# A query bias copied into three of four PSUM banks by ScalarE, with TensorE's bias product kept for the fourth

## What is computed

```
q = softmax(x @ Wq.T + bq, over the 16 channels of a head)
k = softmax(x @ Wk.T + bk, over the 1024 tokens)
v = x @ Wv.T + bv
state = einsum('bhnd,bhne->bhde', k, v);  out = einsum('bhnd,bhde->bhne', q, state)
out = layernorm(out) @ Wo.T + bo
x1 = layernorm(x + out)
```

## Time and profile before

| what | value |
|---|---|
| median of 3 executions | 569.5 us (569.3 to 569.98) |
| the profiled execution's own time | 569.85 us |
| its span | 568.0 us, 10876 instructions |
| DVE, ACT, POOL busy | 502.9, 483.1, 402.7 us |
| PE's granted clock, mean | 0.991 |
| DMA | 46.52 MB, mean 82 GB/s |

### The profile page before, as it was taken

One profiled execution on the slowest core, in us unless ns is written; L12 is line 12 of the kernel. 1 busy time (PEld: TensorE's weight loads), 2 busy tenths in 40 slices (PEclk: granted clock), 3 DMA queues, 4 the chain that ended last, 5 costly groups with the idle time before them and its releaser, 6 DMA issues.

```text
span 568.0 us, 10876 instructions
## 1 busy us (share of the span) xinstructions
PE 541.4 (95%) x3542; PEld 494.0 (87%) x3542; DVE 502.9 (89%) x1276; ACT 483.1 (85%) x951; POOL 402.7 (71%) x390
## 2 busy tenths in 40 slices
PE   6999999999999999988899999999999999999990
PEld 6899999898999989878788998888899888899890
DVE  5888898988899898857587999999999999999986
ACT  4655689799989878877989999999999999999983
POOL 4782979877797987575458776876676776675672
PEclk9999999999999999999999999999999999999996
DMA  8540040230705020250111012222112222100102
GB/s 294 198 149 2 1 186 39 82 141 9 289 1 224 1 113 38 76 200 24 75 38 39 38 37 76 75 74 76 44 33 75 76 74 76 59 18 37 39 38 111
DMA packets 11399, 46.52 MB, mean 82 GB/s; under 512 B 1360, under 2 KB 1744, under 8 KB 9168
## 3 DMA queue, kind: packets, MB, share of 16 engines
q1 hardware_dynamic: 10912, 45.29, 21.9%
q10 hardware_dynamic: 432, 0.54, 0.3%
HBM read 29.02 MB, written 16.81 MB: 81 GB/s over the span
## 4 chain that ended last, share of the span: by engine, by line
PE 74%; DVE 11%; ACT 8%; DMA 2%; issue 2%; POOL 1%; ACTq 0%; DVEq 0%; POOLq 0%
PE ring L1874 20%; PE qps_sps_aps_then_y L1898 20%; PE qps_sps_aps_then_y L1745 7%; PE qps_sps_aps_then_y L1659 7%; PE ring L1687 5%; PE qps_sps_aps_then_y L1764 5%; PE ring L1816 2%; DVE z L1177 2%; PE ring L1791 2%; DVE qsum L1071 1%; PE ring L1779 1%; PE ring L1829 1%; PE qps_sps_aps_then_y L1720 1%; ACT z L746 1%; DMA w_raw<-in_wq_dram 1%
## 5 line engine op out<-in xcount | busy, mean ns | idle before, releaser
L1898 PE MATMUL qps_sps_aps_then_y<-ff_w_over_xc_lo,ff_a_lo_over_qw 128*128 128x258 f32 x512 | 126.5, 283 | 0.0
L1898 PE MATMUL qps_sps_aps_then_y<-ff_w_over_xc_lo,ff_a_hi_over_xc_lo 128*128 128x258 f32 x512 | 126.4, 283 | 0.0
L1874 PE MATMUL ring<-ff_ht_hi_over_qw,t 128*128 128x512 f32 x256 | 105.6, 412 | 0.9 <-DVE ff_ht_lo_over_xc_hi L1249 0.5
L1874 PE MATMUL ring<-ff_ht_lo_over_xc_hi,t 128*128 128x512 f32 x256 | 100.8, 394 | 0.0
L1898 PEld LDWEIGHTS qps_sps_aps_then_y<-ff_w_over_xc_lo,ff_a_hi_over_xc_lo 128*128 128x128 f32 x512 | 96.9, 189 | 3.5
L1898 PEld LDWEIGHTS qps_sps_aps_then_y<-ff_w_over_xc_lo,ff_a_lo_over_qw 128*128 128x128 f32 x512 | 96.7, 189 | 3.4
L1257 DVE SCALAR_TENSOR_TENSOR ff_a_lo_over_qw<-ring,ff_rho,ff_a_hi_over_xc_lo 128x512 fp32r<-128x512 f32 x128 | 91.5, 742 | 5.7 <-ACT ff_a_hi_over_xc_lo L807 4.5
L789 ACT ACTIVATE ring<-ring,bias 128x512 f32<-128x512 f32 x128 | 84.1, 677 | 11.2 <-PE ring L1874 10.2
L522 POOL TENSOR_TENSOR ff_accp_over_xt_lo<-ff_accp_over_xt_lo,ff_sq_over_ek_et_hi 128x512 f32<-128x512 f32 x64 | 84.3, 1317 | 4.7
L805 ACT ACTIVATE ff_sq_over_ek_et_hi<-ring 128x512 f32<-128x512 f32 x128 | 79.1, 618 | 0.5
L807 ACT CAST ff_a_hi_over_xc_lo<-ring 128x512 fp32r<-128x512 f32 x128 | 78.0, 609 | 0.0
(11 more groups left out here) (179 smaller groups left out, 1631.1 us busy)
## 6 DMA issues: line engine op xcount, KB each, us to landing
x_scratch<-z SPq DMA_DIRECT2D x16, 514.0 KB, 2.9
ff_x_over_w_raw_xc<-x_scratch SPq DMA_DIRECT2D x16, 514.0 KB, 4.8
xt<-in_x_tok_dram SPq DMA_DIRECT2D x8, 1024.0 KB, 4.8
out_dram<-ff_z_over_et_lo SPq DMA_DIRECT2D x15, 512.0 KB, 3.5
xc<-in_x_chan_dram SPq DMA_DIRECT2D x6, 1024.0 KB, 6.9
w_raw<-in_w_dram SPq DMA_DIRECT2D x2, 1024.0 KB, 5.4
xc<-in_x_chan_dram SPq DMA_DIRECT2D x2, 512.0 KB, 6.7
ek<-in_x_chan_dram SPq DMA_DIRECT2D x1, 1024.0 KB, 9.3
```

The source lines that it names most:

```text
L1874: mm = nc.tensor.matmul(ff_bank(k, m), t1[:, c, m * P:(m + 1) * P], h[:, k % 2, c], start=(c == 0 and j == 0), stop=(c == CH - 1 and j == 1))
L1898: last = nc.tensor.matmul(ff_yps[:, t, 0:C + 2], a[:, m % DEPTH, t * P:(t + 1) * P], ff_w2[:, m], start=(m == 0 and j == 0), stop=(m == FC ...
```

## The change

ACT copies the bias for pair 2 as well, so that PE makes a bias product for pair 3 only (from batch 1 on). The new copy waits, as L681 has it, until DVE has subtracted pair 0, whose bank pair 2 takes. In ACT's list it is put between `k_exponent(0, 1)` and `pt_high(0, 0)` for batch 1, and in round b between `projected_high(b - 1)` and the second group of normalisations for batch b + 1. The seeded pairs' counts on `q_seed` go from two a batch to three. Nothing else is changed.

```
-SEEDED = (0, 1)
+SEEDED = (0, 1, 2)
...
             chan_hi(2)
             k_exponent(0, 1)
+            q_bias(1, 2)
             pt_high(0, 0)
             pt_high(0, 1)
...
                 normalise(b - 2, 0)
                 projected_high(b - 1)
+                q_bias(b + 1, 2)
                 normalise(b - 2, 1)
                 k_exponent(b, 0)
                 chan_hi(b + 2)
```

## The result

The changed kernel takes **572.38 us** in the median (571.8 to 573.15, 6 runs) where the kernel before takes 569.92: 1.0045 times as long, 95% interval 1.0031 to 1.0059. One of the six executions of the kernel before took 760.9 us, for which the record has no reason; the other five took 569.3 to 570.56, and their median is 569.86. It is slower, by 2.5 us where 1.9 were forecast. Its profiled execution took 572.9 us with a span of 571.0.

The account below looks back on a forecast made before the run. PE's order of work sets a round, with ACT setting its pace at tile 2. Batch 0's 0.6 and rounds 1 to 6 (-0.23, 0.03, 0.51, 0.46, 0, 0.5) sum to +1.9 us: 571.4 from 569.5, range 569.0 to 572.9.

Parts of the forecast that it names:

- main step: From r_hi to the copy of tile 0, ACT has no idle time; the new copy adds 0.51 us, delaying PE.
- batch 0: The copy before pt_high(0, 0) delays a serial chain through to PE's state sum: +0.6 us.
- likeliest case: The forecast itself, whole kernel: slower by +1.2 to +2.6 us, 570.7 to 572.1 us, chance 0.50.
- round 2: Tile 2 comes 0.51 us later, but the state's transpose then waits less for r_f, leaving about +0.03.
- round 5: Tile 2's delay of +0.46 us shrinks to 0 through a shorter wait for r_f.
- round 6: PE's query transposes wait for the exponential of the keys, which ends 0.51 us later: +0.5 us.
- lower bound: Whole kernel: +0.7 us if batch 0 absorbs its part and rounds 4 and 5 have 0.3 more slack.
- the row for tile 2: Rounds 2 to 5: PE's load waits for ACT's copy to z, growing from 0.6 us in 2 times.
- without a gap: Third query pair: its first product follows its predecessor directly, as the copy is in time, by 0.1 us in round 2.
- rival C: Third query pair: the copy itself is late, costing a further 0.2 us in each of 6 rounds; 572.6 us, chance 0.12.
- A: Rounds 2 to 5: ACT has slack, so PE's 1.6 us saving stays whole; 567.9 us, chance 0.11.
- B: Round ends: POOL's pace or shifted DVE-POOL collisions absorb the delays; 569.5 +/- 1.1 us, likeliest 570.2, chance 0.27.

Follow-up runs that it names:

- e1: Kernel before with PE's bias product of pair 2 left out from batch 1 on and no copy in its place: 569.68 us, ratio 0.9999.
- e2: Changed kernel with PE's bias product of pair 2 put back behind the wait for ACT's copy, which it overwrites: 571.96 us, ratio 1.0037.
- e3: Changed kernel without the copy for batch 1, whose pair 2 gets its bias from PE as before: 571.47 us, ratio 1.0024.
- e6: Changed kernel with attention tile 2 of batches 0 to 5 in bank 1 instead of bank 2: 571.36 us, ratio 1.0031.
- e11: Kernel before with pair 2 copies for batches 2 to 7, tile 2 in bank 1, key exponential ahead of the second normalisations: 570.07 us, ratio 1.0009.
- e9: Kernel before without pair 2's bias product or copy, tile 2 in bank 1, key exponential ahead of the second normalisations: 569.67 us, ratio 1.0000.
- e10: Changed kernel with the copy for pair 2 made twice into the same bank, the second waiting for the first: 575.93 us, ratio 1.0110.

## Why the forecast was right, point by point

**Right in its direction and its main step.** ACT's stretch from r_hi to the copy of tile 0 grew by 0.51 us, as worked out from the neighbour's row, and PE waits at its end in rounds 2 to 5 (4 times, where it was 2). PE's removed products are worth nothing where that stretch ends last (e1, e2). The sum was +1.9: 0.6 of batch 0 and 1.27 of the rounds; measured are 0.69 and 1.43. In absolute terms 571.4 was said and 572.38 measured, inside the recorded 569.0 to 572.9 but above the likeliest case's own 570.7 to 572.1: the kernel before measured 0.4 higher than the median that the forecast started from, and the medians differ by more than the stages do (below).

**By its terms** (forecast, measured in us): batch 0 0.6, 0.69; round 1 -0.23, -0.17; round 2 0.03, 0.24; round 3 0.51, 0.48; round 4 0.46, 0.56; round 5 0, -0.14; round 6 0.5, 0.46. None is off by more than 0.14 but round 2's. There I had the wait for r_f take back 0.48 of 0.51. That 0.48 was the wait of the weight load, which runs ahead; what PE's products lose, and so can get back, is in their own rows of the kernel before, for rounds 3 and 6:

```profile
110.78 0.44 PE L1712 MATMUL qps_sps_aps_then_y<-ident,r_f 128*128 128x128 f32 x2 [0.28 <-DVE r_f L1135]
...
207.01 0.44 PE L1712 MATMUL qps_sps_aps_then_y<-ident,r_f 128*128 128x128 f32 x2 [0.44 <-DVE r_f L1135]
```

With 0.28 in place of 0.48, round 2 would have been 0.51 - 0.28 = 0.23 (measured 0.24), and with 0.44 round 5 0.02 (measured -0.14). The whole sum would have been about 2.1, as measured. This was the one mis-sized term. The lower bound had a slip as well: it took 0.3 off for round 5, which the sum had at 0 already, so it should have been +1.0 and not +0.7.

**Batch 0** went as traced: seed at 30.24 - 0.29 = 29.95 (29.96 forecast), cast 30.47 (30.46), state sum 35.97 (35.9). e3 shows the term standing alone.

**Wrong: the row for tile 2**, "over 2 us in 4 times", "0.5 us or more each". It is 1.6 in 4, 0.4 each. The step that failed is the sentence that a wait of the query transposes for the exponential appears in round 6. It appears in five of the six rounds, before tile 2 and off the same delay, and takes most of it there; e6 shows that tile 2 alone accounts for 0.46 us. The length of the round came out right all the same, and in part by luck, because both waits hang on the same 0.51 us in one stretch of ACT and the second only gets what the first leaves. In the earlier trace rows the exponential was the later one in round 6 by 0.05 us; I didn't look how near it was in rounds 2 to 5, and the e1 run, with a PE that is 0.23 earlier, shows it waited for in rounds 2, 3 and 6.

**Wrong in part: that the third pair's first product follows "without a gap".** The product's load waits for it in rounds 2, 3 and 6, 0.9 us together, and in round 2, where I had it in time by 0.1, PE loses 0.1, so of rival C a small part is true. e11 suggests that it is what stays when the other two waits are gone; that was not shown.

**The rivals.** A fell with e1. B, absorption by POOL's pace, holds in two rounds only, as forecast; the shift between DVE and POOL that it spoke of did not show in the changed kernel, but it is what the rows of e9 look like. C was wrong for one copy; with two, PE waits for the seed in every round (e10).

**The remaining 0.4 us** between the 2.1 of the stages and the 2.5 of the medians isn't explained. e2, with nearly the same batch 0 and rounds, has 571.96, 0.4 under after, and the changed kernel's six runs spread over 1.35 us, so it may be no more than that spread.

## What to carry to other kernels

Before work is moved from the fullest engine to one with 15% idle, read where that idle time lies. Here ACT had no idle row between the place of the insertion and two results that PE came for within 0.05 us: rounds 3, 4 and 6 paid nearly the whole duration, rounds 2 and 5 got half or all of it back from a wait that stood behind, and the work taken off PE bought only waiting.
A cheap first run is the removal alone (e1): if leaving work out altogether gains nothing, there is nothing that moving it could be expected to gain. Price a wait that may give time back by the row of the product, not by that of its weight load. When one wait is taken away and the time stays, look for the next result on the same delayed chain, ahead of it in the program's order and not only behind it.

## What the runs showed of the hardware

The price of a small operation in a full stream was its distance to the next one's start: 0.51 us for a copy whose own row says 0.58, 0.23 us for a product whose row says 0.39, and the product's held when it was put back (1.1 us for 5, e2). A second copy that waits for the first took 0.62 (e10). PE resumed 0.05 to 0.06 us after the end of ACT's instruction that it waited for, whichever that was (the copy to z, the exponential's last part, the new copy). A wait in the row of weight loads was longer than PE's own at the same place: 0.48 against 0.28 us and 0.64 against 0.44 for r_f in the kernel before, 0.69 against 0.37 for the exponential in round 6 after.
The start of the program, up to batch 1's first query product, was 1.29 us shorter (e6) to 0.67 us longer (e9) than before's in single profiled executions, and one store of z took 3.09 us in one execution and 3.60 in another. Both are as large as the terms of this change, so single executions were compared by stage and not by their ends.
